# A two-layer transformer kernel: who writes the fp16 low halves of the dense layers, and who adds their biases

## The chip, the core and the metric

The kernel runs on one core of one Trainium2 chip. The metric is device time in microseconds (us) for one execution; the median of three runs is 1115.12 us. A core has TensorE (matrix multiplication, PE in the profile), VectorE (DVE), ScalarE (ACT), GpSimd (POOL), and SyncE (SP), which here only issues transfers. Each engine works through its own program in order, and a semaphore wait in one program holds up all that stands behind it there.

## What is computed

Four batches of 512 tokens of width 256 go through two layers. The change touches the first one. In the reference, cut to that part:

```python
q_prob, k_prob = _prob(q), _prob(k)
log_ratio = jnp.log(q_prob) - jnp.log(k_prob)
sid = jnp.einsum('bnd,bmd->bnm', q_prob - k_prob, log_ratio)
attn = jax.nn.softmax(-sid / D ** 0.5, axis=-1)
attn_feat = jnp.einsum('bnm,bmd->bnd', attn, v)
f_diff = (v - attn_feat) @ W_diff.T + b_diff + q
h = _layernorm(f_diff, ln_g, ln_b)
mlp = gelu(h @ W1.T + b1) @ W2.T + b2            # width 1024 inside
out = _layernorm(mlp + f_diff, ln_g, ln_b)
...
x = x + out
h = _layernorm(x) @ W_in + b_in                  # then 8 routed experts, top 2
logits = h @ W_gate + b_gate
```

The dense products run as pairs of fp16 halves: a value is rounded to fp16 (the high half), the rest, value minus high half, is rounded to fp16 too (the low half), and TensorE adds high·high, high·low and low·high in PSUM.

## The kernel before

A batch passes these stages, each a function in the code: `pre(b)` and `s_exp(b)` (the attention scores from DT and LT, their exponentials ET), `rest(b)` (attention output Q at L822 and L1621, its LayerNorm to UZ at L1629, transposes, scaled and shifted to UZ at L1635, which is h transposed, then its halves HT), `mlp(b)` (W1 at L843, the gelu twice by ScalarE at L1296, to G in f32 and GT in fp16, the low half of GT at L2154 by GpSimd, W2 at L855, then the second LayerNorm to XB and X on VectorE, L1660 and L1665), and `moe_pre(b)` (LayerNorm of X to XN at L1704, its transposes XTH, the gate at L909, W_in at L916, with the bias at L1728, HL as two halves at L1350 and L2186, the rows written to memory at L2188, then the ranks and places of the tokens in the experts: rf, Qh, Rh, L970). Meanwhile `kv` prepares keys and values of the batches (VAB at L1685), and `split` turns the first layer's expert weights into halves: tag "m" for w1 (w1h, w1l), tag "p" for w2 (w), 16 chunks each, loaded by SyncE into buffers SR, SRs and SRW, high half by ScalarE (L1332), low half by VectorE (L1697). A buffer may be loaded again only when its low half is made. GpSimd also forms LQ−LC (L2118) and prepares the next batch's Q and X (L2125, L2127, L2128), once ScalarE has written LC.

GT has eight blocks (hc 0 to 7), G a ring of four buffers. PSUM has eight banks: a ring of three, Y, for tiles of 256 columns, a ring of two, T, and a ring of three, Sx. `fill(...)` issues matmuls on the identity, identh, into a bank that nobody reads (L780).

What order the work has on each engine is fixed when the program is built. Each stage is a generator for each engine, and `order()` advances them: `weave` by one step each in turn, `beside` the side ones at a rate per step of the main one. In the loop over b = 0..3, `rest(b)` goes together with `pre(b+1)`, `mlp(b-1)`, and steps of `moe_pre`; `mlp(3)` comes last, beside moe_pre(2) and the split "p", then moe_pre(3), the route and the 39 tiles of the experts. The experts begin with the copies xt (L1887), products with w1 (L1022), ScalarE's m, VectorE's mh and ml, and products with w.

## Time and profile before

| | before |
|---|---|
| median of 3 runs (lowest, highest) | 1115.12 us (1114.61, 1117.5) |
| the profiled execution | 1118.6 us, of which span 1116.8 us |
| mean granted TensorE clock | 0.920 |
| busy in the span: PE, DVE, ACT, POOL | 970.6, 740.1, 482.3, 284.9 us |
| first layer's attention and dense part | 0 to about 388 us |

The span reaches from the first to the last instruction. Busy times are sums over instructions of one engine; an engine that is idle has a releaser, the instruction of another engine whose semaphore ended the idle time. All durations below are of the one profiled execution.

### The profile page before, as it was taken

What the parts mean: (1) busy time and instruction counts of PE and PEld (TensorE: products, weight loads), DVE (VectorE), ACT (ScalarE), POOL (GpSimd) and SP (SyncE); (2) the same over time, 40 slices, a digit from 0 to 9 for tenths busy, and PEclk for the clock granted to TensorE, in tenths of its full rate; (3) what the DMA queues carried; (4) which work ended last, traced back from release to release, by engine and by line L of the source; (5) the groups of instructions that cost most, each with busy time, mean ns of one, the idle gap of its engine ahead of it and who ended that gap; (6) DMA issues with size and microseconds to landing.
All of it is one profiled execution on the core that took longest, in us unless ns stands there. A gap on an engine that the chain in (4) does not pass through costs nothing.

```text
span 1116.8 us, 20681 instructions
## 1 busy us (share of the span) xinstructions
PE 970.6 (87%) x6905; PEld 583.9 (52%) x6905; DVE 740.1 (66%) x1945; ACT 482.3 (43%) x1058; POOL 284.9 (26%) x246
## 2 busy tenths in 40 slices
PE   6979798969898799999999776888988988896995
PEld 3646374637465488778885442332333333242774
DVE  4483757684878666666663468587676866646796
ACT  4353736343433244444442320444666666641432
POOL 1333523524220233444331001100010001102473
PEclk9999899998998899999999997787998989778999
DMA  9442020003535411111112688142346007332341
GB/s 297 153 132 114 1 76 1 20 13 101 132 95 170 150 50 50 49 50 49 50 45 100 153 150 153 40 59 31 67 86 106 2 21 189 104 130 81 102 130 35
DMA packets 70242, 98.68 MB, mean 88 GB/s; under 512 B 8796, under 2 KB 57183, under 8 KB 67712
## 3 DMA queue, kind: packets, MB, share of 16 engines
q1 hardware_dynamic: 60000, 61.67, 20.6%
q0 software_dynamic: 10144, 35.69, 11.8%
q8 instruction: 63, 1.03, 0.4%
q14 instruction: 35, 0.29, 0.1%
HBM read 71.04 MB, written 27.15 MB: 88 GB/s over the span
## 4 chain that ended last, share of the span: by engine, by line
PE 57%; DVE 25%; DMA 7%; ACT 5%; issue 3%; POOL 1%; SPq 0%; POOLq 0%; ACTq 0%; DVEq 0%
PE pb L1022 12%; PE pb L1039 8%; DVE MX L1992 5%; PE pb L1129 4%; PE pb L1040 4%; PE pb L855 3%; PE pb L780 3%; DMA QS<-qd 3%; PE pb L786 2%; PE pb L1107 2%; PE pb L1153 2%; PE pb L865 2%; PE pb L822 2%; PE pb L809 2%; ACT EX L1442 2%
## 5 line engine op out<-in xcount | busy, mean ns | idle before, releaser
L1992 DVE TENSOR_REDUCE MX<-pb 128x1 f32<-128x512 f32 x256 | 158.3, 681 | 45.3 <-PE pb L1107 44.9
L1442 ACT ACTIVATE EX<-pb 128x512 f32<-128x512 f32 x256 | 137.0, 599 | 117.1 <-PE pb L1153 116.1
L1385 ACT ACTIVATE m<-pb,b1m 128x128 f32<-128x128 f32 x404 | 115.3, 369 | 163.9 <-PE pb L1022 163.9
L780 PE MATMUL pb<-identh 128*128 128x512 f16 x558 | 141.8, 412 | 21.6 <-DVE UZ L1635 10.2
L1022 PE MATMUL pb<-xt,w1h 128*128 128x128 f16 x1616 | 155.0, 220 | 1.5 <-issue 1.5
L1039 PE MATMUL pb<-w,mh 128*128 x404 | 149.3, 379 | 7.1 <-DVE ml L1897 7.0
L1022 PEld LDWEIGHTS pb<-xt,w1h 128*128 x1616 | 119.7, 98 | 37.9 <-issue 2.2
L1022 PE MATMUL pb<-xt,w1l 128*128 128x128 f16 x808 | 111.8, 220 | 0.0
L1040 PE MATMUL pb<-w,ml 128*128 x404 | 110.1, 273 | 0.0
L780 PEld LDWEIGHTS pb<-identh 128*128 128x128 f16 x558 | 56.8, 104 | 97.6 <-issue 25.4
L1107 PE MATMUL pb<-KS,QS 48*128 48x512 f32 x256 | 70.0, 531 | 21.6 <-DVE MX L1992 11.4
L1129 PE MATMUL pb<-EX,VA 128*32 128x512 f32 x512 | 85.9, 736 | 1.1 <-ACT OS L1243 1.0
L1153 PE MATMUL pb<-QS,KS 49*128 49x512 f32 x256 | 76.9, 508 | 7.6 <-ACT EX L1442 6.3
L2209 POOL DMA_INDIRECT outs<-ob,di x39 | 38.7, 991 | 137.1 <-DVE ob L1912 137.1
L1895 DVE CAST mh<-m 128x512 f16<-128x512 f32 x101 | 50.0, 496 | 33.5 <-ACT m L1385 33.4
L1897 DVE TENSOR_TENSOR ml<-m,mh 128x512 f16<-128x512 f32 x101 | 69.9, 692 | 3.5
L2201 POOL DMA_INDIRECT xr<-rows,gi x62 | 61.3, 988 | 34.5 <-issue 17.2
L1107 PEld LDWEIGHTS pb<-KS,QS 48*128 48x128 f32 x256 | 28.8, 209 | 71.5 <-issue 43.4
L1153 PEld LDWEIGHTS pb<-QS,KS 49*128 49x128 f32 x256 | 32.5, 208 | 61.4 <-issue 41.7
L2154 POOL TENSOR_TENSOR GT<-G,GT 128x512 f16<-128x512 f32 x32 | 42.0, 1321 | 88.0 <-ACT GT L1296 87.8
L1022 PEld LDWEIGHTS pb<-xt,w1l 128*128 x808 | 63.0, 98 | 0.1
L1887 DVE COPY xt<-pb 128x512 f16<-128x512 f16 x62 | 26.2, 423 | 48.0 <-PE pb L1005 47.8
(322 smaller groups left out, 1612.5 us busy)
## 6 DMA issues: line engine op xcount, KB each, us to landing
SR<-in_w1m SPq DMA_DIRECT2D x20, 512.0 KB, 5.4
SR<-in_w2m SPq DMA_DIRECT2D x14, 512.0 KB, 4.8
KS<-kd SPq DMA_DIRECT2D x48, 128.0 KB, 5.6
SRW<-in_w2m SPq DMA_DIRECT2D x10, 512.0 KB, 5.2
QS<-qd POOLq DMA_DIRECT2D x18, 256.0 KB, 9.6
kd<-KHL POOLq DMA_DIRECT2D x8, 512.0 KB, 6.6
vd<-VAB POOLq DMA_DIRECT2D x4, 1024.0 KB, 4.3
rows<-HL POOLq DMA_DIRECT2D x8, 512.0 KB, 3.6
```

The lines of the kernel that those rows point to most:

```text
L780: pe.matmul(r.ahead().ap[:, 0:S], identh[:, :], identh[:, :].unsqueeze(1).to_broadcast([128, 4, 128]), start=True, stop=True)
L1022: ins = pe.matmul(k.ap[:, h4 * TOK:(h4 + 1) * TOK], wt[:, bass.ds(regs[j], 128)], M.xt[j % 2][:, xc, :], start=i == 0, stop=i == 5)
L1039: pe.matmul(k.ap, h, M.w2[hc][:, bass.ds(regs[j] * 4, 2 * D)], start=hc == 0, stop=False)
L1040: ins = pe.matmul(k.ap[:, 0:D], l, M.w2[hc][:, bass.ds(regs[j] * 4, D)], start=False, stop=hc == hc_n - 1)
L1107: pe.matmul(k.ap, QS[b % 3][64 * j:64 * j + 48, s, t * 128:(t + 1) * 128], KS[b % 2][64 * j:64 * j + 48, s, :], start=True, stop=True).the ...
L1129: ins = pe.matmul(box["o"].ap[32 * i:32 * i + 32, :], VA[b % 2][:, kc, 4 * g + i, :], EX[(m + i // 2) % len(EX)][:, i % 2, :], start=kc == ...
L1153: pe.matmul(k.ap, KS[b % 2][64 * j:64 * j + 49, s, kc * 128:(kc + 1) * 128], QS[b % 3][64 * j:64 * j + 49, s, :], start=True, stop=True).t ...
L1385: ins = act.activation(M.m32[x % 2][:, h4, :], k.ap[:, h4 * TOK:(h4 + 1) * TOK], M.func, bias=M.b1[:, bass.ds(reg + 4 * g + h4, 1)], scale ...
L1442: act.activation(EX[m % len(EX)][:, i, :], k.ap, ACT.Exp, scale=0.25).then_inc(k.out, 1)
L1897: v.tensor_tensor(l[:, :, :], m[:, :, :], h[:, :, :], ALU.subtract).then_inc(*c.up(f"mid{L}"))
L1992: v.tensor_reduce(mx[:, t, 2 * s + j:2 * s + j + 1], k.ap, AX.X, ALU.max).then_inc(k.out, 1)
L2201: pool.indirect_dma_start(out=M.xr[j % XR[L]][:, :], out_offset=None, in_=M.rows, in_offset=bass.IndirectOffsetOnAxis(ap=r.gi[:, j:j + 1]. ...
```

## The change

1. The low halves of GT are made by VectorE instead of GpSimd, in VectorE's program one block behind the gelu (`low_half`, `GL = 1`).
2. The bias b2, which GpSimd added to Q for a whole batch, is put in by a matmul of `ones` with b2a that opens each PSUM tile of mlp; b_in likewise by a matmul that ends each W_in tile.
3. The high half of HT is made by ScalarE out of PSUM instead of by VectorE from UZ, the low half by VectorE instead of GpSimd. The high half of HL is made by ScalarE out of PSUM for each tile instead of for the batch, the low half by VectorE instead of GpSimd.
4. Order: `LATE` delays the steps of moe_pre and of the split by six in b = 2 and 3; in the last batch, eight steps of mlp(3) go beside moe_pre alone, and then the rest beside moe_pre and the split at 2.0 each. The fills in moe_pre(2), place(1) and place(2) are 6, 4 and 4 matmuls instead of 46, 14 and 28.

The core of the diff (before's and after's line numbers in the heads):

```diff
@@ -30,7 +30,9 @@
 PRES = 0, 0, 13, 13
+LATE = 0, 0, 6, 6
 RP = 3
+GL = 1
 BANK = {i: i for i in range(8)} | {"p0": 0, "p2": 2}
@@ -476,13 +478,16 @@
                 weave(chain(p["pre"](b + 1), p["s_exp"](b + 1)) if b + 1 < NB else None, p["rest"](b),
-                      p["mlp"](b - 1) if b else kvs, None if b else sp0, islice(pres, PRES[b]), islice(sp1, 16) if b == 3 else None)
+                      p["mlp"](b - 1) if b else kvs, None if b else sp0, chain(pause(LATE[b]), islice(pres, PRES[b])),
+                      chain(pause(LATE[b]), islice(sp1, 16)) if b == 3 else None)
                 if b == 0:
...
             sp1 = chain(sp1, p["split"]("p"))
-            beside(p["mlp"](NB - 1), (pres, 2.0), (sp1, 1.8), drain=False)
+            m3 = p["mlp"](NB - 1)
+            beside(islice(m3, 8), (pres, 1.0), drain=False)
+            beside(m3, (pres, 2.0), (sp1, 2.0), drain=False)
             beside(last, (pres, 1.0), (islice(sp1, 16), 1.14), drain=False)
@@ -831,7 +836,7 @@
             def mlp(b):
-                w.wait_ge(sem("h_hi"), b + 1)
+                w.wait_ge(sem("h_hi"), 2 * (b + 1))
                 w.wait_ge(sem("h_lo"), b + 1)
@@ -847,13 +852,16 @@
                     w.wait_ge(*k.before)
+                    w.wait_ge(sem("d_wp"), 7 * 16)
+                    w.wait_ge(sem("ones"), 1)
+                    pe.matmul(k.ap[:, 0:D], ones[0:int(WS), :], b2a[0:int(WS), :], start=True, stop=False)
                     for hc in range(8):
...
                             ins = pe.matmul(k.ap[:, 0:D], GT[hc][:, i, t * 128:(t + 1) * 128], W2x[x][:, hc * D:(hc + 1) * D],
-                                            start=hc == 0 and n == 0, stop=hc == 7 and n == 2)
+                                            start=False, stop=hc == 7 and n == 2)
                     ins.then_inc(k.full, 1)
@@ -894,7 +902,7 @@
                 w.wait_ge(sem("d_wb"), 9 * 16)
-                fill(T, (0, 5, 46, 64)[b])
+                fill(T, (0, 5, 6, 64)[b])
                 w.wait_ge(sem("xn"), b + 1)
@@ -913,8 +921,8 @@
                     for c in range(2):
-                        ins = pe.matmul(kh.ap[:, 0:D], xt[:, c, t * 128:(t + 1) * 128], Win[:, c, :], start=c == 0, stop=c == 1)
-                    ins.then_inc(kh.full, 1)
+                        pe.matmul(kh.ap[:, 0:D], xt[:, c, t * 128:(t + 1) * 128], Win[:, c, :], start=c == 0, stop=False)
+                    pe.matmul(kh.ap[:, 0:D], ones[0:1, :], bin_[0:1, :], start=False, stop=True).then_inc(kh.full, 1)
                     if t % 2:
@@ -961,7 +969,7 @@
             def place(r, b, y):
-                fill(y, ((0, 14, 28, 24), (0, 0, 2, 8))[r.L][b])
+                fill(y, ((0, 4, 4, 24), (0, 0, 2, 8))[r.L][b])
                 k = y.take()
@@ -1279,7 +1287,12 @@
                 yield from pause(2 + RP)
-                T.skip(2)
+                hi = HT[b % 2][:, 0, :, :].rearrange("p c (t n) -> p c t n", t=4)
+                for c in range(2):
+                    k = T.take()
+                    w.wait_ge(*k.mm)
+                    act.activation(hi[:, c], k.ap.rearrange("p (t n) -> p t n", t=4), ACT.Identity, scale=pp[:, c:c + 1], bias=pp[:, 2 + c:3 + c]
+                                   ).then_inc(sem("h_hi"), 1)
                 yield
@@ -1341,13 +1354,13 @@
                 yield
+                w.wait_ge(sem("d_hl0"), 16 * b)
                 for t in range(4):
                     kh = Y.take()
+                    w.wait_ge(*kh.mm)
+                    act.activation(HL[:, t, 0:D], kh.ap[:, 0:D], ACT.Copy).then_inc(sem("x_hi0"), 1)
                     if t % 2:
                         yield
-                w.wait_ge(*kh.ev)
-                w.wait_ge(sem("d_hl0"), 16 * b)
-                act.activation(HL[:, :, 0:D], XN[:, :, :], ACT.Copy).then_inc(sem("x_hi0"), 1)
                 Y.skip(1)
@@ -1631,23 +1644,32 @@
                     k = T.take()
-                    w.wait_ge(*k.mm)
+                    w.wait_ge(sem("h_hi"), 2 * b + cc + 1)
                     v.tensor_scalar(z[:, :, cc * 128:(cc + 1) * 128], k.ap.rearrange("p (t n) -> p t n", t=4), pp[:, cc:cc + 1], pp[:, 2 + cc:3 + cc],
...
                 zc = z[:, :, :].rearrange("p t (c n) -> p c t n", c=2)
-                hi = HT[b % 2][:, 0, :, :].rearrange("p c (t n) -> p c t n", t=4)
+                hi, lo = (HT[b % 2][:, i, :, :].rearrange("p c (t n) -> p c t n", t=4) for i in range(2))
                 for cc in range(2):
-                    ins = v.tensor_copy(hi[:, cc], zc[:, cc])
-                ins.then_inc(*c.up("h_hi"))
+                    ins = v.tensor_tensor(lo[:, cc], zc[:, cc], hi[:, cc], ALU.subtract)
+                ins.then_inc(*c.up("h_lo"))
                 yield
...
                 q = Q[b % 3]
+                ups = []
+
+                def low_half(hc):
+                    w.wait_ge(*ups[hc].ev)
+                    v.tensor_tensor(GT[hc][:, 1, :], G32[hc % 4][:, :], GT[hc][:, 0, :], ALU.subtract).then_inc(*c.up("g_lo"))
+
                 for hc in range(8):
-                    Sx.take()
-                    yield
-                w.wait_ge(sem("fb"), b + 1)
+                    ups.append(Sx.take())
+                    if hc >= GL:
+                        low_half(hc - GL)
+                    yield
+                for hc in range(8 - GL, 8):
+                    low_half(hc)
                 o = []
@@ -1699,7 +1721,6 @@
                 sc = ln_stats([X[:, 4 * b + t, :] for t in range(4)], lnm[b % 2], [(sem("x1"), b + 1)] * 4)
-                w.wait_ge(sem("x_lo0"), b)
                 for t in range(4):
@@ -1724,8 +1745,8 @@
                     k = Y.take()
-                    w.wait_ge(*k.mm)
-                    v.tensor_tensor(XN[:, t, :], k.ap[:, 0:D], bin_[:, :], ALU.add).then_inc(k.out, 1)
+                    w.wait_ge(sem("x_hi0"), 4 * b + t + 1)
+                    v.tensor_tensor(HL[:, t, D:2 * D], k.ap[:, 0:D], HL[:, t, 0:D], ALU.subtract).then_inc(k.out, 1)
                     if t % 2:
@@ -2135,23 +2156,11 @@
                 Y.skip(4)
-                yield from pause(1 + RP)
-                q = Q[b % 3]
-                w.wait_ge(sem("z"), b + 1)
-                pool.tensor_tensor(q[:, :, :], q[:, :, :], b2a.unsqueeze(1).to_broadcast([128, 4, D]), ALU.add).then_inc(sem("fb"), 1)
-                yield
-                w.wait_ge(sem("h_hi"), b + 1)
-                zc = UZ[:, :, :].rearrange("p t (c n) -> p c t n", c=2)
-                hi, lo = (HT[b % 2][:, i, :, :].rearrange("p c (t n) -> p c t n", t=4) for i in range(2))
-                for c in range(2):
-                    ins = pool.tensor_tensor(lo[:, c], zc[:, c], hi[:, c], ALU.subtract)
-                ins.then_inc(sem("h_lo"), 1)
-                yield
+                yield from pause(3 + RP)
 
...
                 for hc in range(8):
-                    w.wait_ge(*Sx.take().ev)
-                    pool.tensor_tensor(GT[hc][:, 1, :], G32[hc % 4][:, :], GT[hc][:, 0, :], ALU.subtract).then_inc(sem("g_lo"), 1)
+                    Sx.skip(1)
                     yield
@@ -2179,12 +2188,12 @@
                 yield
+                ks = []
                 for _ in range(2):
-                    Y.skip(2)
-                    yield
-                w.wait_ge(sem("x_hi0"), b + 1)
-                pool.tensor_tensor(HL[:, :, D:2 * D], XN[:, :, :], HL[:, :, 0:D], ALU.subtract).then_inc(sem("x_lo0"), 1)
-                w.wait_ge(sem("x_lo0"), b + 1)
+                    ks += [Y.take(), Y.take()]
+                    yield
+                for k in ks:
+                    w.wait_ge(*k.ev)
                 pool.dma_start(E0.rows[b * S:b * S + S].rearrange("(t p) d -> p t d", p=128), HL[:, :, :]).then_inc(sem("d_hl0"), 16)
```

How it moves instructions, at three places. The first is GpSimd's program from mlp(1) to the preparation of the last batch; HT_138 and the GT are halves, Q_140 and X belong to the next batch. Before:

```order
L2147 TENSOR_TENSOR HT_138<-UZ,HT_138 128x512 x2
L2154 TENSOR_TENSOR GT_151<-G_1_143,GT_151 128x512
L2154 TENSOR_TENSOR GT_152<-G_2_144,GT_152 128x512
L2154 TENSOR_TENSOR GT_153<-G_3_145,GT_153 128x512
L2118 TENSOR_TENSOR LQ<-LQ,LC 128x4x128 x2
L2186 TENSOR_TENSOR HL<-XN,HL 128x4x256
L2188 DMA rows<-HL 128x4x512
L2125 TENSOR_TENSOR Q_140<-Q_140,VW_134 128x1024
L2127 TENSOR_TENSOR Q_140<-Q_140,bc 128x1024
L2128 TENSOR_TENSOR X<-X,bc 128x1024
```

After, from the batch before on (L2139 is L2118 of before, L2146 to L2149 are L2125 to L2128):

```order
L2139 TENSOR_TENSOR LQ<-LQ,LC 128x4x128 x2
L2146 TENSOR_TENSOR Q_137<-Q_137,VW_133 128x1024
L2148 TENSOR_TENSOR Q_137<-Q_137,bc 128x1024
L2149 TENSOR_TENSOR X<-X,bc 128x1024
L2139 TENSOR_TENSOR LQ<-LQ,LC 128x4x128 x2
L2146 TENSOR_TENSOR Q_140<-Q_140,VW_134 128x1024
L2148 TENSOR_TENSOR Q_140<-Q_140,bc 128x1024
L2149 TENSOR_TENSOR X<-X,bc 128x1024
```

No GT, HT or HL is left between them, and the four writes of rows stand behind all of the batches' preparations.

The second is VectorE's program in the same mlp(1): UZ is h transposed, lgz the gate's result, GT_150 to GT_153 are the last four blocks. Before:

```order
L1585 TENSOR_SCALAR XB<-TC,r_107 128x256 x4
L1635 TENSOR_SCALAR UZ<-pb,pp 128x4x128 x2
L1641 CAST HT_138<-UZ 128x512 x2
L1592 SCALAR_TENSOR_TENSOR TQ<-TQ,r_107,XB 128x256 x4
L1713 TENSOR_TENSOR lgz<-pb,bgate 128x32
L1717 MAX top<-lgz 128x8 x4
```

After, up to the LayerNorm of moe_pre (its 13 rows to XN are left out between the two pieces):

```order
L1598 TENSOR_SCALAR XB<-TC,r_107 128x256 x4
L1648 TENSOR_SCALAR UZ<-pb,pp 128x4x128 x2
L1654 TENSOR_TENSOR HT_138<-UZ,HT_138 128x512 x2
L1664 TENSOR_TENSOR GT_150<-G_0_142,GT_150 128x512
L1664 TENSOR_TENSOR GT_151<-G_1_143,GT_151 128x512
```

```order
L1725 TENSOR_SCALAR XN<-X,mvm_172,ntm_174 128x256 x4
L1605 SCALAR_TENSOR_TENSOR TQ<-TQ,r_107,XB 128x256 x4
L1664 TENSOR_TENSOR GT_152<-G_2_144,GT_152 128x512
L1664 TENSOR_TENSOR GT_153<-G_3_145,GT_153 128x512
L1677 SCALAR_TENSOR_TENSOR Q_136<-pb,Q_136 128x256 x4
```

XN, which stood well ahead of Q_137's LayerNorm, has moved behind GT_151, and behind TQ the last two low halves and the mlp's own LayerNorm (sto) come before lgz.

The third is VectorE's program where the experts begin; the w are low halves of w2, SRW and SR the buffers. Before:

```order
L1887 COPY xt_0_232<-pb 128x512
L1887 COPY xt_1_233<-pb 128x512
L394 TENSOR_LOAD tei_2_76
L1697 SCALAR_TENSOR_TENSOR w_0_5_225<-SRW_186,w_0_5_225 128x4x256
L1697 SCALAR_TENSOR_TENSOR w_0_5_225<-SRW_187,w_0_5_225 128x4x256
L1697 SCALAR_TENSOR_TENSOR w_0_6_226<-SRW_185,w_0_6_226 128x4x256
L1697 SCALAR_TENSOR_TENSOR w_0_6_226<-SRW_186,w_0_6_226 128x4x256
L1697 SCALAR_TENSOR_TENSOR w_0_7_227<-SRW_187,w_0_7_227 128x4x256
L1697 SCALAR_TENSOR_TENSOR w_0_7_227<-SRW_185,w_0_7_227 128x4x256
L1895 CAST mh_0_239<-m_0_0_237 128x512
```

After:

```order
L1908 COPY xt_0_232<-pb 128x512
L1908 COPY xt_1_233<-pb 128x512
L396 TENSOR_LOAD tei_2_76
L1719 SCALAR_TENSOR_TENSOR w_0_2_222<-SRW_186,w_0_2_222 128x4x256
L1719 SCALAR_TENSOR_TENSOR w_0_2_222<-SRW_187,w_0_2_222 128x4x256
L1719 SCALAR_TENSOR_TENSOR w_0_3_223<-SR_163,w_0_3_223 128x4x256
L1719 SCALAR_TENSOR_TENSOR w_0_3_223<-SR_164,w_0_3_223 128x4x256
L1719 SCALAR_TENSOR_TENSOR w_0_4_224<-SR_162,w_0_4_224 128x4x256
L1719 SCALAR_TENSOR_TENSOR w_0_4_224<-SRW_185,w_0_4_224 128x4x256
L1719 SCALAR_TENSOR_TENSOR w_0_5_225<-SRW_186,w_0_5_225 128x4x256
L1719 SCALAR_TENSOR_TENSOR w_0_5_225<-SRW_187,w_0_5_225 128x4x256
L1719 SCALAR_TENSOR_TENSOR w_0_6_226<-SRW_185,w_0_6_226 128x4x256
```

Two more rows of w follow there, and then mh and ml. Six w stood between xt and mh before, twelve do now, and four instead of ten are left ahead of xt.

## Rows read from the trace of the kernel before

**Rows 1.** Busy time of each engine in three stretches (us, instructions), sum over six.
```profile
60.00:120.00 60.00, 52.72 (x213) 32.69 (x212) 37.44 (x104) 30.61 (x68) 22.30 (x17) 0.94 0.33 114
...
231.00:320.00 89.00, 74.05 (x431) 44.43 (x430) 68.50 (x223) 36.77 (x51) 33.26 (x22) 0.92 0.34 95
...
sum 388.00, PE 330.88 PEld 208.55 DVE 259.48 ACT 166.12 POOL 126.14; mean PE 55.15 PEld 34.76 DVE 43.25 ACT 27.69 POOL 21.02
```

**Rows 2.** TensorE's waits, 110 to 375 us: for whom, total, times, longest.
```profile
PE pb L855 <- POOL GT L2154: 7.3, 3, 6.2
PE pb L780 <- DVE UZ L1635: 6.3, 1, 6.3
PE pb L786 <- DVE XN L1704: 5.7, 2, 3.5
```

**Rows 3.** Groups by form, 0 to 388 us: busy us, mean ns, idle before.
```profile
L780 PE MATMUL pb<-identh 128*128 128x512 f16 x347 | 87.4, 411 | 19.2 <-DVE UZ L1635 10.2 <-DVE identh L1551 7.6 <-DVE a L1864 1.4
...
L916 PE MATMUL pb<-Win,XTH 128*128 128x256 f32 x64 | 16.9, 418 | 0.0
...
L2154 POOL TENSOR_TENSOR GT<-G,GT 128x512 f16<-128x512 f32 x32 | 42.0, 1321 | 88.0 <-ACT GT L1296 87.8
```

**Rows 4.** Timeline of TensorE, 312 us: start, us, instruction, count.
```profile
312.06 6.21 PE L780 MATMUL pb<-identh 128*128 128x512 f16 x28
```

**Rows 5.** Timelines of VectorE (three rows) and GpSimd (last row): start, us.
```profile
123.72 5.09 DVE L1585 TENSOR_SCALAR XB<-TC,r 128x256 f32<-128x256 f32 x4
...
183.07 1.38 DVE L1585 TENSOR_SCALAR XB<-TC,r 128x256 f32<-128x256 f32 x4
...
211.33 2.41 DVE L1814 TENSOR_SCALAR Qh<-iotah,qf 128x128 f16<-128x128 f16 x1
...
211.34 2.35 POOL L2127 TENSOR_TENSOR Q<-Q,bc 128x1024 f32<-128x1024 f32 x1
```

**Rows 6.** The page's part 5, one of its groups.
```profile
L1897 DVE TENSOR_TENSOR ml<-m,mh 128x512 f16<-128x512 f32 x101 | 69.9, 692 | 3.5
```

**Rows 7.** Timelines, 190 to 233 us: ScalarE, TensorE (four rows), VectorE (two).
```profile
190.54 2.06 ACT L1263 ACTIVATE LC<-TC,r 128x256 f32<-128x256 f32 x4
...
197.18 0.94 PE L855 MATMUL pb<-W2x,GT 128*128 128x256 f16 x6
...
207.14 2.78 PE L855 MATMUL pb<-W2x,GT 128*128 128x256 f16 x24
...
212.94 7.13 PE L809 MATMUL pb<-DT,LT 128*128 128x512 f32 x16 [0.69 <-ACT LT L1243]
...
231.16 2.10 PE L843 MATMUL pb<-HT,W1x 128*128 128x512 f16 x9
...
219.31 1.40 DVE L1524 BATCH_NORM_STATS2 sto<-Q 128x6 f32<-128x256 f32 x4
...
225.25 1.67 DVE L1665 SCALAR_TENSOR_TENSOR X<-XB,nto,X 128x256 f32<-128x256 f32 x4
```

**Rows 8.** Timelines of VectorE and TensorE, first batch.
```profile
77.06 5.49 DVE L1592 SCALAR_TENSOR_TENSOR TQ<-TQ,r,XB 128x256 f32<-128x256 f32 x4
...
82.94 1.13 PE L890 MATMUL pb<-Wqkv,KVC 128*128 128x256 f32 x4 [2.16 <-DVE VAB L1685]
```

**Rows 9.** Timeline of TensorE, mlp(0).
```profile
135.09 0.82 PE L855 MATMUL pb<-W2x,GT 128*128 128x256 f16 x3 [6.20 <-POOL GT L2154]
```

**Rows 10.** Chain that ended last, 370 to 390 us.
```profile
375.50 0.42 DVE xt L1887
...
376.12 1.24 DVE w L1697
...
379.89 5.24 DMA SRW<-in_w2m
...
385.15 1.07 ACT w L1332
...
388.03 0.70 DVE ml L1897
```

## The prediction

> **What bounds the kernel now.** The change touches only the first third of the program, so I cut that stage (0 to 388 us) into stretches: TensorE is busy 330.88 of 388 us, VectorE 259.48 [rows 1]. The other 57 us of TensorE are waits, and the list of its waits says for whom: three times for the low halves of GT by GpSimd (7.3 us), once for UZ (6.3 us), twice for XN (5.7 us) [rows 2]. Some of its busy time is no work either: 347 instructions, 87.4 us, multiply by identh only to fill waits [rows 3]; a run of 28 of them takes 6.21 us [rows 4], 0.22 each. So TensorE's useful work and the chain through VectorE, ScalarE and GpSimd bound the stage in turns.
>
> The timelines of two engines side by side show what makes that chain slow. Four XB operations of VectorE took 5.09 us while GpSimd added a bias, and 1.38 us in the batch where it did not. Where GpSimd makes three additions in a row, VectorE's Qh of 128 columns takes 2.41 us beside one of 2.35 us [rows 5]. So one operation of GpSimd holds up one of VectorE, then lets one pass. The Trainium skill says the same (SBUF — State Buffer, "Who interferes with whom": both engines share a port pair that one of them locks, and a VectorE instruction with two inputs in SBUF contends for it). The trace agrees in these rows. The rule speaks against this change in one respect: the low halves become VectorE operations with both inputs in SBUF, so GpSimd operations that stay can hold them up. What that costs here is worked out from rows below (C).
>
> **The change part by part**
>
> *Work sums.* GpSimd loses 32 GT halves (42.0 us) [rows 3], and its HT, Q-bias and HL operations. VectorE gains the 32 subtractions, an operation that it has not run in this stage. The nearest row is ml, a subtraction of the same shape and types, 0.692 us [rows 6]; four operations of 256 columns with two inputs take 1.67 us [rows 7], so 0.84 for 512 is the upper bound with nothing between, and beside a GpSimd operation up to 2.4 more [rows 5]. I take 0.69, 22 us in all. TensorE gains 32 bias matmuls of 256 f32 columns. Win's have that shape: 64 records, two for a matmul of the program, 16.9 us [rows 3], 0.53 each, lower clock included; and L809's, twice as wide, take 7.13 us for eight [rows 7], so 0.45. The cheapest of 256 columns, f16, take 2.78 us for 24 [rows 7], 0.12. I take 0.43 (0.12 to 0.53), 13.8 us together. TensorE loses 74 fills, 74 × 0.22 = 16.3 us, which are worth something only where the wait that they cover is gone. ScalarE gains eight reads of PSUM of 0.6 to 0.7 us.
>
> *A, first batch (60 to 105 us).* GpSimd's Q bias and HT low are gone. VectorE's TQ took 5.49 us beside them [rows 8] for four operations that take 1.67 clean [rows 7], and behind TQ stands the VAB for which TensorE waits 2.16 us at 82.94 [rows 8]. 5.49 − 1.67 = 3.8 us come off; HT low costs VectorE 2 × 0.69 instead of the cast's 2 × 0.42, 0.5 back, but no longer waits behind z for both halves, which I count 0.4: +3.7. The 2.16 us of that wait and fills ahead of it are what TensorE can save; late next is the transpose of the next batch's TQ, which moves with it. The clock was granted at 0.94 over 60 to 120 us [rows 1], so 3.6 us went to a lower clock, in a stretch behind such a wait; I count +0.8 of it, between 0 and 1.8: **+4.5** (3.7 to 5.5).
>
> *B, mlp(0) (120 to 149).* TensorE waits 6.20 us for the GT half that GpSimd writes last before 135.09 [rows 9]. VectorE will have it some 4.4 us earlier. But halves 6 and 7 wait for ScalarE, 2 × 0.57 us later for HT, and GpSimd's own work of that batch (L2118 twice, L2125, L2127), until now queued behind the GT halves, starts as soon as LC is written and holds up VectorE's low halves. I get the first tile's end at 138.5 to 140.5 instead of 140.9, less 3 × 0.43 for the biases of the other three: **−0.5** (−2.5 to +1).
>
> *C, mlp(1) with moe_pre(0) (174 to 231).* The largest loss. LC is written from 190.54 to 192.60 [rows 7]; with XTH and the wait for it, some 4 us, out of ScalarE's way, and HT and its PSUM reads in it, I get 188.6, an estimate. GpSimd has nothing else left in its queue then: L2118 twice (half width), L2125, L2127, L2128 are four times 2.3 = 9.2 us back to back, where until now the GT halves parted them. VectorE will at 188 be starting XN ×4, TQ ×4 and the two last low halves: 1.4 + 1.67 + 2 × 0.69 = 4.4 us, all of them of the kind that is held up. 188 + 4.4 + 9.2 = 201.6 us for the last low half, where GpSimd's was there for TensorE's 197.18 [rows 7]. The first tile ends at 202.1 instead of 198.1, and the fourth 3 × (2.6 + 0.43) later, at 211.2; before it ended at 209.9, with Win already done inside.
>
> XN's transposes, gate and Win now stand behind the four tiles, ahead of L809. Three banks of PSUM go round here: the third Win tile waits until the gate's result is read, the fourth for the first HL. VectorE reaches the gate only after Q (0.42) and the LayerNorm of the mlp output, from 219.31 to 226.92 = 7.6 us [rows 7], which now stands ahead of it; then top-8 and one-hots (an estimate from fourteen short instructions, 2.0), HL 0.4, the last Win with its bias 0.9: 11.3, with semaphores 11.5. L809 starts at 222.7 instead of 212.94, 9.8 later. From there to W1 at 231.16 it took 18.2 [rows 7]; rf, Qh and Rh no longer meet GpSimd and the Q that L822 waits for is there, so 16.2 at best, 2.0 back. C is −7.8 with the full lock. Without it the first tile ends at 198.5, and C is −4. Some of the five may find VectorE reading PSUM: **−7.0** (−9.4 with 1.6 more of low clock, to −4).
>
> *D, the rest up to the experts (231 to 388).* All removed fills stand here: of 14, 46 and 28, 4, 6 and 4 are left, 16.3 us off TensorE. Added are 8 biases of mlp(2) and mlp(3) and 12 of Win, 20 × 0.43 = 8.6. Net 7.7 us. The longest waits for UZ (6.3) and XN (3.5) [rows 2] may shorten, but VectorE, busy 68.50 of 89 us from 231 to 320 [rows 1], gets 16 × 0.69 = 11 us more. I let 1.2 of the 9.8 come off: xt, the copy of the first expert tile, comes 8.9 us earlier (0 to 17.5).
>
> Against this stands the tail. Now six w splits stand on VectorE between the copies of xt and the first mh: three of 1.24, a load of 5.24, ScalarE's part (1.07) and VectorE's of the last, so that ml begins at 388.03, 13 us behind the first xt [rows 10]. In the changed order twelve stand there, and loads run six chunks ahead at first, then three: chunk 12 is loaded only when chunk 9's low half is done (xt + 0.6 + 6 × 1.24 = 8.1), lands at 13.3 and is split by 15.6; chunk 15 waits for chunk 12's buffer, 5.24 + 1.07 + 1.24 more, 23.2; with mh and ml **25**. That is 11.8 more than now against 8.9 less: **−3** (−11.8 to +5.7). What hides the splits now is VectorE's idle time before the route; behind xt nothing does.
>
> *Sum.* 4.5 − 0.5 − 7.0 − 3.0 = −6.0, slower by 6.0. The profiled execution took 1118.6 us (its span 1116.8); with the change 1124.6. The median of the three runs, 1115.12, is 3.5 below it: **1121 us**.
>
> **The rivals**
>
> *Faster: VectorE keeps up.* GpSimd's five operations find VectorE reading PSUM, so C is −4, and UZ and XN are so early that both waits in D go: 4.5 + 0.5 − 4 + 5.6 = +6.6, **1108.5 us**. For it: most collisions seen are with operations that the change removes. Against: the twelve splits in the tail. It wins from where xt comes some 15 us earlier. Chance 0.31.
>
> *No change.* C without the lock and a tail that eats D: 4.5 − 0.5 − 4 − 1 = −1, **1116 us**. Here too belongs that the change does not do what it says: TensorE waits for VectorE's low halves as long as it did for GpSimd's. 0.19.
>
> *Clearly slower.* VectorE becomes the bound in D and xt comes only 3 us earlier: 4.5 − 0.5 − 7 − 9 = −12, **1127 us**. 0.14.
>
> *The forecast*: 0.36, with a range of its own of 1118 to 1124.
>
> **How the numbers follow.** A measurement of this kernel tells some 0.3%, 3.3 us, from no change. Under 1111.8 lies the first rival, 0.31; the second within, 0.19; the forecast and the last above, 0.50. The range reaches from the first rival's time to just past the last one's, 1108 to 1128.
>
> **What the profile after would show.** Right: the VAB tile at 79 us; no wait for GT near 130; the first tile of mlp(1) ending near 202, with XN, TQ or low halves beside five GpSimd additions taking over 2 us each; L809 of that batch starting near 223; ml 25 us behind xt. Wrong: low halves all near 0.69 us; L809 before 216; the w splits already done when mh's input is there; xt over 12 us earlier.

## The result, and the profile after

The changed kernel takes 1136.15 us (median of four runs, 1132.33 to 1139.86) against 1116.31 us before: ratio 1.0172, 95% interval 1.0136 to 1.0209, so between 19 and 20 us more. The forecast was 1121 us in a range of 1108 to 1128; the direction was right, the size was not, and the time lies 8 us above the range.

The head of the changed kernel's page (span; busy us, share of the span and instructions of each engine):

```profile
span 1136.5 us, 20661 instructions
...
PE 983.4 (87%) x6895; PEld 590.9 (52%) x6895; DVE 736.6 (65%) x1977; ACT 490.2 (43%) x1078; POOL 214.6 (19%) x198
```

GpSimd gives up 70 us. VectorE, which takes over its subtractions, is not busier at all (736.6 for 740.1 us), and TensorE is busy 12.8 us longer although 74 fills are gone. The first ml of the experts stands at 407.38 us for 388.03 before [rows 10], 19.35 us later, and the rest of the program is the same to within half a microsecond. So all of it is in the stage that I had cut into A to D. Marks in the timelines divide it: the end of L822 (L827 in the changed kernel) in each loop turn, at 114.8, 168.6 and 231.3 us before and 108.9, 167.2 and 241.4 after, the first xt, 374.9 and 386.3, and the first ml.

| stretch | forecast | found |
|---|---|---|
| A, to L822 of batch 1 | 4.5 less | 5.8 less |
| B, mlp(0) | 0.5 more | 4.4 more |
| C, mlp(1) with moe_pre(0) | 7.0 more | 11.5 more |
| D, to the first xt | 8.9 less | 1.3 more |
| D, xt to ml | 11.8 more | 7.9 more |
| sum | 6.0 more | 19.3 more |

These are readings of one execution each. Two later kernels (e3 and e5) differ from the changed one only in D, and their A, B and C took 0.9 and 1.9, 0.2 and 0.3, and 1.8 and 1.8 us more than its. So a difference of less than some 2 us in one stretch says nothing by itself.

A is a little better than its range of 3.7 to 5.5; TensorE's wait for VAB after the change (compare [rows 8]):

```profile
78.80 1.13 PE L898 MATMUL pb<-Wqkv,KVC 128*128 128x256 f32 x4 [2.15 <-DVE VAB L1707]
```

It comes 4.1 us earlier (3.7 forecast), and the clock was granted in full from 60 to 120 us, where it was at 0.94 [rows 1]. The wait itself is still there: what stands behind it moved with it.

B was to be a draw and lost 4.4 us. TensorE's waits for low halves in mlp(0), two of three:

```profile
132.05 0.50 PE L863 MATMUL pb<-W2x,GT 128*128 128x256 f16 x3 [3.81 <-DVE GT L1664]
134.79 0.82 PE L863 MATMUL pb<-W2x,GT 128*128 128x256 f16 x3 [2.25 <-DVE GT L1664]
```

VectorE makes these two halves from 129.36 on and needs 5.38 us for them instead of 1.28, while GpSimd adds from 126.84 to 136.94 without a pause.

C is the same collision, which the forecast had described for this place. The timelines of VectorE, GpSimd and TensorE after the change:

```profile
187.52 1.12 DVE L1529 TENSOR_TENSOR ntm<-ntm 128x4 f32<-128x4 f32 x1
188.67 1.19 DVE L1531 SCALAR_TENSOR_TENSOR ntm<-ntm 128x4 f32<-128x4 f32 x1
189.90 7.31 DVE L1725 TENSOR_SCALAR XN<-X,mvm,ntm 128x256 f32<-128x256 f32 x4
197.12 1.66 DVE L1605 SCALAR_TENSOR_TENSOR TQ<-TQ,r,XB 128x256 f32<-128x256 f32 x4
198.71 1.28 DVE L1664 TENSOR_TENSOR GT<-G,GT 128x512 f16<-128x512 f32 x2
...
187.33 2.51 POOL L2139 TENSOR_TENSOR LQ<-LQ,LC 128x512 f32<-128x512 f32 x2 [50.39 <-ACT LC L1271]
189.80 2.16 POOL L2146 TENSOR_TENSOR Q<-Q,VW 128x1024 f32<-128x1024 f32 x1
192.05 2.34 POOL L2148 TENSOR_TENSOR Q<-Q,bc 128x1024 f32<-128x1024 f32 x1
194.34 2.39 POOL L2149 TENSOR_TENSOR X<-X,bc 128x1024 f32<-128x1024 f32 x1
...
199.44 1.46 PE L863 MATMUL pb<-W2x,GT 128*128 128x256 f16 x6 [10.76 <-DVE GT L1664]
```

Five operations of GpSimd, 9.4 us in a row, meet five of VectorE: two of four elements per partition that otherwise take 0.16 us and here take 1.12 and 1.19, and three of the four XN (the shortest of the four took 0.40 us, the middle ones about 2.3). As soon as GpSimd is through, TQ and both low halves run at their clean durations, 1.66 and 0.64 each. ScalarE had the last GT block ready at 190.99; VectorE makes its low half at 199.99. TensorE sits 10.76 us where it sat not at all before. The Trainium skill (SBUF — State Buffer, "Who interferes with whom") lets a VectorE instruction with two inputs in SBUF contend, and says that the order of issue and not the shape decides who is held up; the 1.12 and 1.19 us of the small ones, which have two such inputs, agree. The condition of two inputs does not cover everything that was held up: XN, like XB and Qh in [rows 5], is a TENSOR_SCALAR that reads one tensor and small columns of scalars. That these rows confirm the condition, as the prediction says, is more than they show; they show the lock.

TensorE's waits for low halves and XN, of the changed kernel, up to the first xt (compare [rows 2]):

```profile
PE pb L863 <- DVE GT L1664: 23.4, 5, 10.8
...
PE pb L791 <- DVE XN L1725: 3.8, 2, 2.9
```

The wait for XN shrank from 5.7 to 3.8 us, and that of the fills for UZ, 6.3 us before, no longer occurs in this stretch; the wait for the low halves tripled, 7.3 to 23.4 us. Of the 23.4, 7.4 are in mlp(0) and 10.8 in mlp(1), both beside GpSimd. The rest is another thing, in mlp(2):

```profile
262.66 0.82 PE L863 MATMUL pb<-W2x,GT 128*128 128x256 f16 x3 [5.23 <-DVE GT L1664]
```

GpSimd does nothing there. ScalarE wrote that block by 256.08, but VectorE's program has the LayerNorm of moe_pre(1), XN and a split of w1 ahead of the low half, which begins at 261.93. Those 5.2 us come from the order of VectorE's program.

The bias matmuls are what the forecast had too cheap. The groups of the changed kernel by form (two records for one matmul of the program), and what of them lies in D, with the granted clock in the third number from the right; the first row from 241 us is b2's (L857), the other two are b_in's (L925):

```profile
L925 PE MATMUL pb<-bin__55,ones 1*128 1x256 f32 x32 | 14.8, 550 | 0.0
L857 PE MATMUL pb<-bc,ones 64*128 64x256 f32 x32 | 12.7, 481 | 0.0
...
241.00:330.00 89.00, 6.09 (x16) 2.56 (x16) 0.88 0.27 78
...
241.00:330.00 89.00, 7.12 (x16) 2.95 (x16) 0.88 0.27 78
330.00:386.00 56.00, 4.87 (x8) 1.99 (x8) 0.79 0.42 129
```

27.5 us for 32, not 13.8. TensorE's timeline shows one at either clock, two records each; the next matmul starts 0.63 us after it at the higher one and 1.15 us at the lower:

```profile
217.78 0.69 PE L925 MATMUL pb<-bin__55,ones 1*128 1x256 f32 x2
218.41 1.13 PE L924 MATMUL pb<-Win,XTH 128*128 128x256 f32 x4
...
288.63 1.22 PE L925 MATMUL pb<-bin__55,ones 1*128 1x256 f32 x2
289.78 2.07 PE L924 MATMUL pb<-Win,XTH 128*128 128x256 f32 x4
```

D has two parts, and the change acts on them in opposite ways. Up to the run of 64 fills (330.7 us before, 334.0 after), where most of the removed fills and 16 of the 20 biases lie, it is 6.8 us shorter, at a clock of 0.89 for 0.93. From there to xt it is 8.1 us longer, at 0.77 for 0.81. Nearly all of the 8.1 is in the four W_in tiles, which with their biases take 13.1 us (from 356.86 to the fills at 369.98) instead of 6.0: four biases at the lower clock are 4.6 of it, and the products themselves take 2.0 us a tile instead of 1.4.

The tail after the change, from the chain that ended last (compare [rows 10]):

```profile
386.33 0.42 DVE xt L1908
...
387.20 1.24 DVE w L1719
...
393.50 1.24 DVE w L1719
394.75 3.66 DMA SRW<-in_w2m
...
398.49 1.06 ACT w L1345
...
399.65 1.24 DVE w L1719
400.90 3.58 DMA SRW<-in_w2m
...
404.50 1.06 ACT w L1345
...
405.66 1.24 DVE w L1719
...
407.38 0.70 DVE ml L1918
```

The chain is the one forecast, link by link; ml begins 21 us behind xt instead of 25, since the loads took 3.6 us, not the 5.24 of before.

### The profile page after: what moved, and what is told of

Its sections match the earlier page's. It is cut to its first block, busy times and chain, and to the rows that moved or that the text cites. A ratio compares the mean times of both kernels' runs of the same rounds, so it can differ in the third digit from the quotient of the medians.

```text
span 1136.5 us, 20661 instructions
## 1 busy us (share of the span) xinstructions
PE 983.4 (87%) x6895; PEld 590.9 (52%) x6895; DVE 736.6 (65%) x1977; ACT 490.2 (43%) x1078; POOL 214.6 (19%) x198
## 4 chain that ended last, share of the span: by engine, by line
PE 59%; DVE 24%; ACT 7%; DMA 5%; issue 3%; POOL 0%; SPq 0%; POOLq 0%; DVEq 0%; ACTq 0%
PE pb L1030 12%; PE pb L1047 8%; DVE MX L2013 5%; PE pb L1048 4%; PE pb L1137 4%; PE pb L863 4%; PE pb L791 3%; PE pb L827 2%; PE pb L814 2%; PE pb L873 2%; PE pb L1115 2%; PE pb L785 2%; PE pb L1161 2%; ACT EX L1455 2%; PE pb L924 2%
## 5 line engine op out<-in xcount | busy, mean ns | idle before, releaser
L1047 PE MATMUL pb<-w,mh 128*128 x404 | 150.2, 381 | 13.8 <-DVE ml L1918 13.7
L1030 PE MATMUL pb<-xt,w1h 128*128 128x128 f16 x1616 | 157.4, 222 | 1.4 <-issue 0.8
L785 PE MATMUL pb<-identh 128*128 128x512 f16 x484 | 118.9, 400 | 11.0 <-DVE identh L1564 6.5
L785 PEld LDWEIGHTS pb<-identh 128*128 128x128 f16 x484 | 48.1, 102 | 72.2 <-issue 17.1
L1137 PE MATMUL pb<-EX,VA 128*32 128x512 f32 x512 | 81.4, 706 | 1.0 <-ACT OS L1251 1.0
L863 PE MATMUL pb<-W2x,GT 128*128 128x256 f16 x384 | 51.5, 294 | 23.5 <-DVE GT L1664 23.4
```

The costliest lines, as they stand in the source:

```text
L785: pe.matmul(r.ahead().ap[:, 0:S], identh[:, :], identh[:, :].unsqueeze(1).to_broadcast([128, 4, 128]), start=True, stop=True)
L863: ins = pe.matmul(k.ap[:, 0:D], GT[hc][:, i, t * 128:(t + 1) * 128], W2x[x][:, hc * D:(hc + 1) * D], start=False, stop=hc == 7 and n == 2)
L1030: ins = pe.matmul(k.ap[:, h4 * TOK:(h4 + 1) * TOK], wt[:, bass.ds(regs[j], 128)], M.xt[j % 2][:, xc, :], start=i == 0, stop=i == 5)
L1047: pe.matmul(k.ap, h, M.w2[hc][:, bass.ds(regs[j] * 4, 2 * D)], start=hc == 0, stop=False)
L1137: ins = pe.matmul(box["o"].ap[32 * i:32 * i + 32, :], VA[b % 2][:, kc, 4 * g + i, :], EX[(m + i // 2) % len(EX)][:, i % 2, :], start=kc == ...
```

## Experiments

Twelve kernels. Each ratio is to the kernel before on the same chip; stretches and marks are those of the kernel's one profile.

**e1: GpSimd's additions held back.** In GpSimd's mlp:

```diff
                 for hc in range(8):
                     Sx.skip(1)
+                    if hc == 7:
+                        w.wait_ge(sem("g_lo"), 8 * (b + 1))
                     yield
```

> The changed kernel, with GpSimd's remaining additions held until the batch's last low half of GT is made. If the collision of these five additions with VectorE's XN costs what the trace shows, TensorE's wait of 10.76 us at L863 in mlp(1) falls to about 3 us, XN takes 1.4 us instead of 7.3, and the kernel is about 7 us faster than the changed one (1129). Rival, that the additions are only needed later and their delay comes back at the transposes of LQ or at L814: 0 to 2 us.

1125.52 us, ratio 1.0079 (1.004 to 1.0117), about 10 us less than the changed kernel, where 7 were expected. In its timelines:

```profile
184.39 1.38 DVE L1725 TENSOR_SCALAR XN<-X,mvm,ntm 128x256 f32<-128x256 f32 x4
185.69 1.67 DVE L1605 SCALAR_TENSOR_TENSOR TQ<-TQ,r,XB 128x256 f32<-128x256 f32 x4
187.28 1.28 DVE L1664 TENSOR_TENSOR GT<-G,GT 128x512 f16<-128x512 f32 x2
...
188.01 1.10 PE L863 MATMUL pb<-W2x,GT 128*128 128x256 f16 x6 [2.86 <-DVE GT L1664]
...
188.64 2.49 POOL L2139 TENSOR_TENSOR LQ<-LQ,LC 128x512 f32<-128x512 f32 x2 [45.88 <-DVE GT L1664]
```

XN is back at 1.38, the wait at 2.86. One wait added to GpSimd's program, and C falls from 74.2 to 66.0 us and B from 58.3 to 52.6. The rival, that the additions' delay comes back later, is out: it doesn't. The lock was over half of the loss, in two places, mlp(0) and mlp(1).

**e2: no bias matmuls.** b2 and b_in are left out of the computation, nothing else is changed.

```diff
-                    pe.matmul(k.ap[:, 0:D], ones[0:int(WS), :], b2a[0:int(WS), :], start=True, stop=False)
...
-                    pe.matmul(kh.ap[:, 0:D], ones[0:1, :], bin_[0:1, :], start=False, stop=True).then_inc(kh.full, 1)
```

> The changed kernel without both bias matmuls: b2 and b_in are left out of the computation, nothing else changes. 32 matmuls of 0.63 us at the higher clock and 1.22 at the lower (trace of the changed kernel) are 20 to 24 us of TensorE. If TensorE is the bound where they stand (the 16 in the W2 tiles and 12 of the 16 in the W_in tiles), the kernel is 14 to 20 us faster than the changed one, 1116 to 1122. Rival, that VectorE's chain sets the pace and the biases stand in waits: under 6 us.

1115.83 us, ratio 0.998 (0.9945 to 1.0016): about 20 us less. Up to xt, D takes 127.2 us instead of 144.9, so 17.7 of it is there, about as much as the matmuls were busy in that stretch (18.1). The rival, under 6 us, is out. The match does not hold part by part: up to the 64 fills 10.4 us go, where the biases were busy 13, and behind them 7.3, where they were busy 4.9 and the clock rose from 0.77 to 0.85. And outside D the other twelve biases are worth little: B is 1.9 and C 1.8 us shorter without them, and the wait for the low halves in mlp(1) is then 11.5 us.

**e3: the last batch in before's order.**

```diff
-            m3 = p["mlp"](NB - 1)
-            beside(islice(m3, 8), (pres, 1.0), drain=False)
-            beside(m3, (pres, 2.0), (sp1, 2.0), drain=False)
+            beside(p["mlp"](NB - 1), (pres, 2.0), (sp1, 1.8), drain=False)
```

> The changed kernel with the last batch in before's order: splits beside all of mlp(3) at 1.8, so that six w stand behind xt instead of twelve. The tail theory: ml starts 12 to 13 us behind xt instead of 20.8, 8 us gained, less what the six splits cost ahead of xt (7.4 us of VectorE at most): 3 to 8 us faster than the changed one. Rival, that VectorE is the bound ahead of xt too: 0.

1135.56 us, ratio 1.0159 (1.0105 to 1.0213): no difference from the changed kernel that these intervals could show. VectorE's timeline there:

```profile
395.58 0.42 DVE L1906 COPY xt<-pb 128x512 f16<-128x512 f16 x1 [1.45 <-PE pb L1011]
...
409.72 0.69 DVE L1916 TENSOR_TENSOR ml<-m,mh 128x512 f16<-128x512 f32 x1
```

ml is 14.1 us behind xt again instead of 21, as the count of splits says, but xt is 9.3 us later. Of the 9.3, 2.8 stand already ahead of D, where this edit changes nothing; D itself is 6.4 us longer against 6.9 less behind xt. So the time agrees with the rival: the place of the six splits doesn't matter to the sum. The edit also weaves moe_pre(2) and mlp(3) differently, and whether the 6.4 us are the splits or that order is not separated.

**e4: LATE at zero.**

```diff
-LATE = 0, 0, 6, 6
+LATE = 0, 0, 0, 0
```

> The changed kernel with LATE at zero, so that moe_pre(0) is woven into mlp(1) again and moe_pre(1) into mlp(2). If the late order costs, the stretch from mlp(1) to W1 of the last batch is 4 us shorter; but XN and the LayerNorm stand ahead of VectorE's low halves 6 and 7, which would be up to 4 us later. I expect 2 us faster than the changed one, between 3 slower and 6 faster; the rival, that biases and clock are the cause, expects no difference.

1128.71 us, ratio 1.01 (1.005 to 1.015), about 8 us less, somewhat beyond what I had allowed. C falls from 74.2 to 64.2 us. The gate and W_in are back between the mlp tiles, and TensorE's wait for the low halves in it is

```profile
195.72 0.50 PE L863 MATMUL pb<-W2x,GT 128*128 128x256 f16 x3 [1.85 <-DVE GT L1664]
```

since XN had been made earlier and stood in nobody's way when GpSimd began. There is a second reason, in GpSimd's timeline:

```profile
189.89 2.48 POOL L2139 TENSOR_TENSOR LQ<-LQ,LC 128x512 f32<-128x512 f32 x2 [51.64 <-ACT LC L1271]
```

The three larger additions follow only at 208.17, because the write of batch 0's rows, which waits for HL, stands between them and L2139 again. The late order had taken that write out of the way, and with it one more wait. B, where LATE is zero in either kernel, stays at 58.5 us. So LATE acts three times: it moves XN into the collision, it lets three additions start early, and it moves gate and W_in out of TensorE's gaps. The three are not separated here.

**e5: fills back** (46, 14 and 28 instead of 6, 4 and 4).

> The changed kernel with the 74 removed fills back (46, 14 and 28 as before). They are 16.3 us of TensorE's time. If TensorE is the bound between 241 and 386 us, as the run without bias matmuls says (17.8 us less there), the kernel is 10 to 16 us slower than the changed one (1146 to 1152). Rival: the fills stand in waits and keep the clock up (it was granted at 0.79 from 330 to 408 us), so the time is the same or up to 8 us less.

1172.55 us for 1133.08 of before on that chip, ratio 1.0344 (1.0284 to 1.0403), some 19 us more than the changed kernel and 3 more than the upper end of what I expected. ml stands at 423.4 us, 16.0 later, but that this is the 16.3 us of the fills is a coincidence: 4.0 of it stand ahead of D, where nothing differs. In D up to the 64 fills, where the 74 are, 14.7 us are added; from there to xt it is 3.2 us less, at a clock of 0.79 for 0.77. The fills nearly all cost their time, so they cover little any more, and they aren't what the time was lost to. That they keep the clock up is worth 3.2 us at most.

**e6: e1 and e4 together.**

> The changed kernel with both edits that helped alone: GpSimd's additions held behind the last low half (10.6 us faster alone), and LATE at zero (7.4 us faster alone). If the two act on different things, the lock and the order of moe_pre(0) behind the mlp tiles, they add up: 1118. If both are ways of getting XN and the low halves past GpSimd's additions in mlp(1), the second adds at most 2 us: about 1124.

Ratio 1.0044 (1.0011 to 1.0077). Of 0.0093 and 0.0072 alone 0.0128 are left together, between the two expectations. In the profile it isn't even that: ml stands at 393.05, e1's at 392.76. The stretches say where they overlap: C is 64.2 us, as with e4 alone, and B 54.3, near e1's 52.6. In mlp(1) both hold back the same additions, in mlp(0) only e1's edit acts. By how much they overlap is not shown.

**e7: as e6, and b2 added by GpSimd as before.**

> As the run with both edits, and b2 added by GpSimd to Q again, so that 16 bias matmuls leave TensorE (the 16 of b_in stay). 16 x 0.63 = 10 us of TensorE less; GpSimd's 2.35 us addition comes back beside XB and TQ, which cost 4 us once per batch where TensorE waited for it (A). I expect 4 to 8 us less than the run with both edits. Rival: the collision eats the gain, 0.

Ratio 1.0002 (0.9959 to 1.0045); ml at 387.1 instead of 393.05, 6 us less. The addition beside VectorE costs less than 16 f32 matmuls, by 5 to 6 us; the intervals of the two ratios overlap.

**e8: low halves of GT on GpSimd again**, the rest of the change kept.

```diff
+                    w.wait_ge(*Sx.take().ev)
+                    pool.tensor_tensor(GT[hc][:, 1, :], G32[hc % 4][:, :], GT[hc][:, 0, :], ALU.subtract).then_inc(sem("g_lo"), 1)
```

> The changed kernel with the low halves of GT on GpSimd again, the rest as changed. GpSimd's additions are then queued behind the GT halves as before, so the 10.76 us wait in mlp(1) goes, and VectorE has 22 us less; GT halves cost 1.3 instead of 0.69 us and collide with VectorE. If the lock in mlp(0) and mlp(1) is what the move to VectorE cost, it is 5 to 11 us faster than the changed one (1125 to 1131). Rival, that the move is worth having by itself: slower than the changed one.

Ratio 1.0076 (1.0036 to 1.0115), the same as e1's 1.0079. So the main part of the change, who makes the low halves, makes no difference that shows once GpSimd's additions come behind them; what it did was to take the GT halves out of GpSimd's queue, where they had kept the additions back.

**e9: as e7, with b_in in fp16.** A small tile bb of 256 fp16 values per partition holds the high half of b_in in partition 0 and the low half in partition 32, zeros between, prepared once by VectorE; one fp16 matmul with ones (oh) adds both.

```diff
-                    pe.matmul(kh.ap[:, 0:D], ones[0:1, :], bin_[0:1, :], start=False, stop=True).then_inc(kh.full, 1)
+                    w.wait_ge(sem("bb"), 1)
+                    pe.matmul(kh.ap[:, 0:D], oh[0:33, :], bb[0:33, :], start=False, stop=True).then_inc(kh.full, 1)
```

> The run with both edits and b2 on GpSimd, and b_in put into the W_in tiles by one fp16 matmul on two rows (high and low half, prepared once) instead of one in f32. A 256-column fp16 matmul took 0.12 us in a run of them, the f32 one 0.63 to 1.22: 16 x 0.5 to 1.1 = 8 to 17 us of TensorE less, all but four of them where TensorE is the bound. I expect 6 to 10 us less than that run, 0.991 to 0.995 of before. Rival, that the W_in tiles are bound by their readers on ScalarE and VectorE: same as before, 1.000.

Ratio 0.9925 (0.9894 to 0.9956): faster than both kernels, 8 us less than before. ml at 374.65, 12.4 earlier than e7's.

**e10: e6 with both biases in fp16** (b2's halves, times 64, in partitions 64 and 96 of the same tile).

> The changed kernel with GpSimd's additions held behind the last low half, LATE at zero, and both biases put in by fp16 matmuls on two rows. The run without bias matmuls was 0.019 below the changed one, the two edits 0.013; together and less 32 x 0.12 us: 0.988 to 0.992 of before. Rival, that lock and biases hide each other: 0.996.

Ratio 0.9941 (0.9913 to 0.9969), a little less gain than expected (0.988 to 0.992) and a little more than the rival's 0.996, ml at 376.50. The groups by form, b_in's and b2's:

```profile
L927 PE MATMUL pb<-bb,oh 33*128 33x256 f16 x16 | 4.8, 300 | 0.0
...
L858 PE MATMUL pb<-bb,oh 33*128 33x256 f16 x16 | 4.5, 280 | 0.0
```

One record each, 0.29 us, 9.3 us for the 32 in place of 27.5. From e9 it can't be told apart.

**e11: e10 in before's last order.**

> As the last, and the last batch in before's order. With TensorE relieved, VectorE may have room ahead of xt for the six w that the changed order puts behind it, so ml comes 13 us behind xt instead of 21 and xt not later by as much: 2 to 5 us less. If VectorE is the bound there, as in the changed kernel, no difference.

Ratio 0.9941 (0.9908 to 0.9973), equal to e10. xt at 368.64 and ml at 383.17 in its profile for 355.16 and 376.50: again later in front (D by 11.6 us) and shorter behind (6.8). Its profile is of an execution 4 us above its median, so the 6.7 us by which ml is later count for little. The expected 2 to 5 us are a miss, and e3 is confirmed.

**e12: part 1 alone in the kernel before.**

> The kernel before with part 1 alone: low halves of GT by VectorE one block behind. GpSimd's additions L2118 to L2128 follow LC at once and collide in mlp(0) and mlp(1) as in the changed kernel, and the Q bias and HT low halves still collide too. The lock theory: the gain in waits for GpSimd's last halves (7.3 us in all) is lost again, and TensorE waits at L855 in mlp(1) 5 to 9 us: 3 to 9 us slower than before. Rival, that the move helps and another part harms: 3 to 6 us faster.

Ratio 1.0035 (0.9997 to 1.0073): 4 us more, just not clear of none. The lock shows best here, in mlp(0), on the operations in dispute themselves; VectorE, then GpSimd:

```profile
130.57 6.49 DVE L1592 SCALAR_TENSOR_TENSOR TQ<-TQ,r,XB 128x256 f32<-128x256 f32 x4
136.99 5.57 DVE L1651 TENSOR_TENSOR GT<-G,GT 128x512 f16<-128x512 f32 x2
...
131.62 2.85 POOL L2127 TENSOR_TENSOR LQ<-LQ,LC 128x512 f32<-128x512 f32 x2
134.43 2.34 POOL L2134 TENSOR_TENSOR Q<-Q,VW 128x1024 f32<-128x1024 f32 x1
136.85 2.41 POOL L2136 TENSOR_TENSOR Q<-Q,bc 128x1024 f32<-128x1024 f32 x1
139.22 2.78 POOL L2137 TENSOR_TENSOR X<-X,bc 128x1024 f32<-128x1024 f32 x1
```

Two low halves take 5.57 us beside two additions, 1.28 without. B takes 59.7 us for 53.8 before. My rival of a helpful move is out, and so is my figure of 5 to 9 us for one wait in mlp(1): the largest wait at L855 in mlp(1) is 2.1 us and the largest of all 4.2, in mlp(0), where the loss is.

## Why the forecast was right in direction and wrong in size

*What was right.* The lock between GpSimd's additions and VectorE, one for one, its place (XN, TQ and low halves of mlp(1)), its trigger (the additions are no longer queued behind GT halves), and the order of its size. The forecast's times go by the old start of C, and C began 1.4 us earlier, so they are compared from its start: the last low half ready after 33.0 us forecast, 32.8 found; L809, now L814, after 54.1 forecast, 57.3 found. e1 and e12 show the cause. A's gain was right too, 3.7 forecast for VAB and 4.1 found. So was the mechanism of the tail.

*The step that failed first: 0.43 us for a bias matmul.* The sum had 13.8 us for 32; they were busy 27.5. Two things were wrong in it. At the higher clock one takes 0.63, not 0.43: the Win row had said 0.53 on average, and I took a value below it from runs of matmuls that use all 128 rows, then called 0.53 the upper bound. And I priced a term that lies in a stretch of low clock by a duration at the high one; at the lower it is 1.15. In D alone they were busy 18.1 us where the sum had 8.6, and e2, which takes them away, gets 17.7 back there: that is 9.1 of the 10.2 us by which xt was off. e9 and e10 take most of it away and keep the biases.

*The second: B.* The forecast named the lock here too, and then let VectorE have the last half so early that the first tile would end 0.4 to 2.4 us sooner. VectorE reads it 26.7 us after the stretch's start, for 26.4 before: the two last halves took 5.38 us, not 1.28. Behind it the other three tiles took 4.1 us more. Their biases are 2.4 of that, one at the lower clock; 1.3 is the second tile's own products, at the lower clock after TensorE's waits. e1 takes 5.6 us off B with the biases left in, e2 takes 1.9 off without them. So B was lost to the lock, and the forecast's price of it was too low.

*The third: what C had left to lose.* 7.0 was a guess below the full lock's 7.8, "some of the five may find VectorE reading PSUM". None did; and operations of four elements were held up too. Of the 3.7 us beyond the full lock 2.5 are in tiles two to four of mlp(1): 1.1 for their biases and 1.4 for their products, most of it in the tile behind the wait, at the lower clock. The forecast had allowed 1.6 for that clock, but not in its middle. The last 1.2 are too small for one profile. One reading was wrong besides: the last Win tile has two products and not one, and took 1.69 us with its bias where 0.9 was counted. Without the lock the forecast had C at 4 more, and e1 has 3.3.

*The fourth: the tail.* Twelve splits behind xt cost 7.9 us more there, not 11.8. Two loads of 3.6 instead of 5.24 us are 3.2 of the difference, and the 25 us were counted past the start of ml: 23.2 and mh's 0.44 make 23.7. The larger error is the sentence that VectorE's idle time ahead of the route hides the splits. e3 and e11 move six of them back there and gain nothing: what is saved behind xt is lost ahead of it. By these two runs the order of the last batch should have stood in the sum at zero, ahead of xt and behind it together. They don't show which of the two changes in that order takes the time ahead of xt.

*The rivals.* None of the four cases happened: the worst one named VectorE as D's bound. In D up to the 64 fills TensorE was busy 84.0 of 92.6 us and VectorE 66.5, and e2 and e5 move that part by 10.4 and 14.7 us with edits of TensorE's work alone; e3 shows that it isn't TensorE alone. The range was too narrow because its upper end took each term at its middle but D's. With each term at its own worst the prediction's numbers give 3.7 − 2.5 − 9.4 − 11.8 = −20.0, 1135 us, close to the measured time by luck: B, C and D up to xt were each 1 to 2 us worse than their worst, A and the tail better.

## What to carry to other kernels

Before an operation is moved off a shared queue, ask what stood behind it there: the queue was also a wait, and what it held back may now run where it does harm; a wait on one semaphore (e1) keeps the gain. A bias matmul in f32 is not small: 0.63 to 1.15 us against 0.29 for both fp16 halves in one matmul, and in D, where TensorE was busy 128.7 of 144.9 us, twenty of them cost 17.7. Read its price from the whole tile: what stands next to it can get longer too. And before a difference of one stretch is explained, look how far the same stretch differs between profiles in which its code did not change, here up to 2 us. Price each term at the clock of the stretch in which it will lie.

## What the runs showed of the hardware beyond what I expected

- Small VectorE operations are held up by GpSimd as well: four elements per partition took 1.12 and 1.19 us instead of 0.16 beside a GpSimd addition.
- An f32 matmul with one row of weights (K = 1) takes as long as one with 64: 0.63 us for 256 columns at the higher clock, 1.15 at the lower, against 0.43 at the higher one for a Win matmul of 128 rows in a run of them (1.73 for four, e2). It costs more than its own time: a W_in tile without bias, two such matmuls, takes 0.87 us at the higher clock and with it 1.69 (from 319.99 to 321.68 in the changed kernel), a W2 tile 2.62 and 3.35. So one bias is 0.73 to 0.82 us there.
- An fp16 matmul of 33 rows takes 0.29 us, more than the 0.12 of one in a run, and adds 0.32 to a W2 tile (2.94 for 2.62, e10).
- Both operands of an fp16 matmul may lie in partitions 64 to 96: e10 adds b2 so, and four bias halves fit in one tile of 512 bytes per partition.
